# One transformer layer on Trainium2: K's bias added by VectorE in place of a TensorE product per tile and a ScalarE copy

## What is computed

```
h   = layernorm(x) * (1 + ca) + sa
Xn  = layernorm(h) * gamma + beta
Q, K, V = split(Xn @ W_in + b_in)
K, V = rotary(K), rotary(V)                 # first 256 columns
A   = sum over tokens of (K/|K|) * (V/|V|)
Y   = (0.5 * A + 0.5) * Q
x   = x + ga * (Y @ W_out + b_out + h)
x   = x + gb * experts(layernorm(x) * (1 + cb) + sb)   # 8 experts, 2 per token, and a shared one
```

## Time and profile before

| | us |
|---|---|
| median of 3 runs | 775.45 |
| lowest, highest | 774.5, 776.64 |
| the profiled execution, its own time | 775.31 |
| its span in the profile | 773.5 |
| granted clock of TensorE, mean | 0.969 of full speed |

### The profile page before, as it was taken

How to read it: one execution, slowest core, us unless ns; L and a number is a source line. 1 busy time by engine, 2 the same in 40 slices (tenths; PEclk the granted TensorE clock), 3 DMA queues, 4 the chain that set the end, 5 groups by cost and what they waited for, 6 DMA issues and landing times.

```text
span 773.5 us, 10585 instructions
## 1 busy us (share of the span) xinstructions
PE 718.8 (93%) x3812; PEld 590.2 (76%) x3812; DVE 476.6 (62%) x958; ACT 263.6 (34%) x491; POOL 166.2 (21%) x220
## 2 busy tenths in 40 slices
PE   5799999999787698999999997999999999999993
PEld 1477777778565486788787886889898999989892
DVE  3886688537999934335767745284655747465541
ACT  2455255422454314012012022253443525344330
POOL 1233133200111200000000003114335161533404
PEclk9799999999999989999999997999999999999997
DMA  8921211001376721110410404548376674836415
GB/s 298 354 71 54 83 28 42 15 1 44 134 219 217 247 67 47 55 56 0 127 57 15 133 0 125 169 144 173 114 141 135 149 133 143 170 118 106 54 15 69
DMA packets 44107, 83.57 MB, mean 108 GB/s; under 512 B 6969, under 2 KB 15161, under 8 KB 43522
## 3 DMA queue, kind: packets, MB, share of 16 engines
q1 hardware_dynamic: 35106, 62.06, 24.9%
q0 software_dynamic: 8960, 20.98, 15.4%
HBM read 59.93 MB, written 24.40 MB: 109 GB/s over the span
## 4 chain that ended last, share of the span: by engine, by line
PE 72%; DVE 15%; issue 5%; DMA 3%; ACT 2%; POOL 2%; SPq 1%; ACTq 0%; DVEq 0%; POOLq 0%
PE bank L1471 21%; PE bank L1472 20%; PE bank L1473 20%; PE bank L1710 3%; DVE rows L1149 1%; DVE st L960 1%; DVE hx L1161 1%; PE bank L1589 1%; DVE xt L1168 1%; PE bank L1510 1%; DVE gsel L1384 1%; PE bank L1528 1%; DVE ht L1376 1%; DMA ewst<-in_L_ffn_w_up 1%; PE bank L1483 1%
## 5 line engine op out<-in xcount | busy, mean ns | idle before, releaser
L1471 PE MATMUL bank<-ht,ew 128*128 128x320 f32 (+1 forms) x384 | 118.9, 310 | 0.7 <-DVE bc_c L1391 0.7
L1472 PE MATMUL bank<-ht,ew 128*128 128x320 f32 (+1 forms) x384 | 118.6, 309 | 0.0
L1473 PE MATMUL bank<-ht,ew 128*128 128x320 f32 (+1 forms) x384 | 118.2, 308 | 0.0
L1471 PE MATMUL bank<-xt,sgu 128*128 128x512 f32 x176 | 70.3, 400 | 4.6 <-DVE rows L1149 4.6
L607 POOL DMA_INDIRECT out_rows<-y,si x40 | 62.9, 1572 | 48.6 <-DVE y L1406 33.7
L1471 PEld LDWEIGHTS bank<-ht,ew 128*128 128x128 f32 (+1 forms) x384 | 68.7, 179 | 1.6 <-DVE bc_c L1391 1.0
L1472 PE MATMUL bank<-xt,sgu 128*128 128x512 f32 x176 | 69.6, 395 | 0.0
L1473 PE MATMUL bank<-xt,sgu 128*128 128x512 f32 x176 | 69.5, 395 | 0.0
L1472 PEld LDWEIGHTS bank<-ht,ew 128*128 128x128 f32 (+1 forms) x384 | 68.6, 179 | 0.3
L1473 PEld LDWEIGHTS bank<-ht,ew 128*128 128x128 f32 (+1 forms) x384 | 68.7, 179 | 0.0
L596 POOL DMA_INDIRECT picked<-h_d,gi x40 | 39.6, 990 | 97.4 <-PE bank L1710 86.7
(11 more groups left out here) (282 smaller groups left out, 1533.4 us busy)
## 6 DMA issues: line engine op xcount, KB each, us to landing
xring<-in_L_attn_X SPq DMA_DIRECT2D x32, 256.0 KB, 3.4
ewst<-in_L_ffn_w_gate SPq DMA_DIRECT2D x8, 704.0 KB, 4.5
ewst<-in_L_ffn_w_up SPq DMA_DIRECT2D x8, 704.0 KB, 4.3
slots<-in_L_wmod SPq DMA_DIRECT2D x4, 1024.0 KB, 6.3
x_d<-rows SPq DMA_DIRECT2D x16, 256.0 KB, 3.7
h_d<-hx SPq DMA_DIRECT2D x16, 256.0 KB, 2.0
xrow<-x_d SPq DMA_DIRECT2D x16, 256.0 KB, 2.8
out_rows<-xrow SPq DMA_DIRECT2D x16, 256.0 KB, 2.8
```

Source lines behind the costliest of these rows:

```text
L1471: nc.tensor.matmul(dst, a[0], b[0], start=first, stop=False)
L1472: nc.tensor.matmul(dst, a[0], b[1], start=False, stop=False)
L1473: return nc.tensor.matmul(dst, a[1], b[0], start=False, stop=last)
```

## The change

K's product loses its bias product and ends with the 12th. In tile 0 TensorE makes the bias once, as rows for all partitions, in W_BANK, and ScalarE copies it to `kb` (which lies where the bias pairs were). VectorE's new `k_row(t)` adds it to K's bank and writes `ksb`; ScalarE's `k_row` goes. `k_square` reads `ksb` in place of the bank and waits for it. `k_row(t)` stands in VectorE's turn between tokens_lo(t+1) and x_statistics(t+3). TensorE may write K's bank again when `k_row` has read it.

```diff
@@ -180,6 +180,8 @@
                 prod = al2("prod", [P, 2, 3 * ROT])
                 arow = al2("arow", [P, B, ROT])
                 cs = al2("cs", [P, NB, 2, P])
+                with ExitStack() as row_phase:
+                    kb = region(row_phase)("kb", [P, D])
                 bkv = al2("bkv", [P, 2, D], F32R)
                 mrow = al2("mrow", [P, 2, D])
             u = al("u", [P, 2, D])
@@ -256,6 +258,7 @@
         s0_ready = sem("s0_ready")
         w_hi, w_lo = sem("w_hi"), sem("w_lo")
         bias_mm, bias_hi, bias_ready = sem("bias_mm"), sem("bias_hi"), sem("bias_ready")
+        kb_mm, kb_ready = sem("kb_mm"), sem("kb_ready")
         sincos, sinsq = sem("sincos"), sem("sinsq")
         misc_mm, misc_read = sem("misc_mm"), sem("misc_read")
 
@@ -664,17 +667,11 @@
                     act.wait_ge(misc_mm, MISC.index("mod") + 1)
                 nc.scalar.activation(tokens(t, 0), chunked(bank[T_BANKS[t % 2]][:, :]), ACT.Copy).then_inc(t_hi, 1)
 
-            def k_row(t):
-
-                act.wait_ge(k_mm, t + 1)
-                if t >= 2:
-                    act.wait_ge(multiplied, t - 1)
-                nc.scalar.activation(ksb[:, t % 2, :], bank[K_BANKS[t % 2]][:, :], ACT.Copy).then_inc(k_copied, 1)
-
             def k_square(t):
                 if t:
                     act.wait_ge(v_sq, t)
-                nc.scalar.activation(junk[:, :], bank[K_BANKS[t % 2]][:, :], ACT.Square,
+                act.wait_ge(k_copied, t + 1)
+                nc.scalar.activation(junk[:, :], ksb[:, t % 2, :], ACT.Square,
                                      accum_out=nrm[:, t, 0:1]).then_inc(k_sq, 1)
 
             def v_square(t):
@@ -741,7 +738,9 @@
                     v_square(t - 1)
                 if t == NB + 1:
                     a_rows(0)
-                k_row(t)
+                if t == 0:
+                    act.wait_ge(kb_mm, 1)
+                    nc.scalar.activation(kb[:, :], bank[W_BANK][:, :], ACT.Copy).then_inc(kb_ready, 1)
                 if t + 1 < NT:
                     tokens_hi(t + 1)
                 k_square(t)
@@ -1000,6 +999,17 @@
                 dve.wait_ge(bias_hi, i + 1)
                 dve.scalar_tensor_tensor(bkv[:, i, :], bkv[:, i, :].bitcast(F32), nodd[:, :],
                                          bank[(W_BANK, MISC_BANK)[i]][:, :], ALU.mult, ALU.add).then_inc(bias_ready, 1)
+
+            def k_row(t):
+
+                dve.wait_ge(k_mm, t + 1)
+                if t == 0:
+                    dve.wait_ge(kb_ready, 1)
+                else:
+                    dve.wait_ge(multiplied, t)
+                if t >= 2:
+                    dve.wait_ge(k_sq, t - 1)
+                dve.tensor_tensor(ksb[:, t % 2, :], bank[K_BANKS[t % 2]][:, :], kb[:, :], ALU.add).then_inc(k_copied, 1)
 
             def products(t):
 
@@ -1097,6 +1107,7 @@
                     modulated(t + 2)
                 if t + 1 < NT:
                     tokens_lo(t + 1)
+                k_row(t)
                 if t + 3 < NT:
                     x_statistics(t + 3)
                 if t in (8, 9):
@@ -1515,18 +1526,21 @@
 
                 to = bank[(K_BANKS, V_BANKS)[i][t % 2]][:, :]
                 if t >= 2:
-                    pe.wait_ge((k_sq, v_sq)[i], t - 1)
+                    pe.wait_ge((k_copied, v_sq)[i], t - 1)
                 if i == 0:
                     pe.wait_ge(t_lo, t + 1)
                 for k in range(DC):
                     if t == 0:
                         pe.wait_ge(w_lo, DC * i + k + 1)
-                    product3(to, [tokens(t, s)[:, k, :] for s in range(2)], [wkv[:, s, i, k, :] for s in range(2)],
-                             k == 0, False)
+                    last = product3(to, [tokens(t, s)[:, k, :] for s in range(2)], [wkv[:, s, i, k, :] for s in range(2)],
+                                    k == 0, not i and k == DC - 1)
+                if i == 0:
+                    last.then_inc(k_mm, 1)
+                    return
                 if t == 0:
-                    pe.wait_ge(bias_ready, i + 1)
-                nc.tensor.matmul(to, pairs4[:, :].to_broadcast([P, P]), bkv[:, i, :], start=False, stop=True)\
-                    .then_inc((k_mm, v_mm)[i], 1)
+                    pe.wait_ge(bias_ready, 2)
+                nc.tensor.matmul(to, pairs4[:, :].to_broadcast([P, P]), bkv[:, 1, :], start=False, stop=True)\
+                    .then_inc(v_mm, 1)
 
             def misc(name):
 
@@ -1534,6 +1548,7 @@
                 to = bank[W_BANK if name == "cos_a" else MISC_BANK]
                 if n < 2:
                     pe.wait_ge(bias_ready, 2)
+                    pe.wait_ge(kb_ready, 1)
                 else:
                     pe.wait_ge(misc_read, n)
                 if name in ("s1", "c1"):
@@ -1622,6 +1637,10 @@
             bias_row(1)
             for t in range(NT):
                 kv_matmul(t, 0)
+                if t == 0:
+                    pe.wait_ge(bias_ready, 1)
+                    nc.tensor.matmul(bank[W_BANK][:, :], pairs4[:, :].to_broadcast([P, P]), bkv[:, 0, :],
+                                     start=True, stop=True).then_inc(kb_mm, 1)
                 if t + 1 < NT:
                     transposes(t + 1)
                 for name in SLOT_A.get(t, ()):
@@ -1631,7 +1650,7 @@
                     misc(name)
                 if t:
                     weighted_sums(t - 1)
-            pe.wait_ge(k_sq, NT - 1)
+            pe.wait_ge(k_copied, NT)
             pe.wait_ge(v_sq, NT - 1)
             pe.wait_ge(t_lo, NT)
             m_matmul(0, (0,))
```

## The result

| | before | after |
|---|---|---|
| median of 20 runs | 773.91 us | 776.34 us |
| lowest, highest | 772.62, 777.2 | 773.7, 778.04 |
| ratio, 95% interval | | 1.0029 [1.0018, 1.004] |
| span of the profiled execution | 773.5 | 774.9 |

The change costs 0.29%, some 2.2 us, with 0.9 us of uncertainty to either side. 777.6 us had been forecast over a median of 775.4, so +2.2. The cost lies just inside the bound of 0.3% that the prediction drew for "same", but its interval leaves out zero: it is small and real.

The account below looks back on a forecast made before the run. TensorE, busy 93% of the span, was taken to set the loop's time. Removed products -3.45, misc bank stall +1.88 and tiles 8 to 14 +3.77 give +2.20 us: 775.4 + 2.2 = 777.6 us, range 773.4 to 780.3.

Parts of the forecast that it names:

- same: Outcome class: measured time within 0.3% of before, 773.1 to 777.8 us; chance 0.43.
- c1's wait: Sign in tile 1: TensorE waits for ScalarE before c1, near 44.5 us, for 1.9 us.
- three waits for tokens_lo: Sign between 120 and 150 us: TensorE waits for VectorE's tokens_lo by 0.7, 1.4 and 1.4 us.
- The gain: K's bias products removed in tiles 1 to 15: 15 x 0.23 = 3.45 us off TensorE.
- Place 1: Misc bank, tiles 1 to 4: B-slot product waits for ScalarE's read behind the square; 1.88 us stall, tiles 2 to 4 0.
- Place 2: Tiles 8 to 14: VectorE's turn grows from 7.44 to 8.36 us against TensorE's 6.94; stalls 3.77 us.
- late weights: Tile 14: weighted_sums(13) comes some 0.19 us late.
- The sum: End of the loop: -3.45 + 1.88 + 3.77 = +2.20 us.
- Carried over whole: Behind the loop: TensorE has no idle time from 158 to 190 us, so all +2.20 us reaches the total.
- (1): Rival: TensorE's clock falls after idle gaps at the loop's start, costing 1.7 us more, 779.3 us; chance 0.22.
- (2): Rival: the square does not hold ScalarE, both places stay hidden, all 3.45 us come through, 772.0 us; chance 0.08.
- (3): Rival: only one place bites; only the second 775.7 us, only the first 773.9 us; chance 0.18 together.

Follow-up runs that it names:

- e1: Kernel before with K's bias product left out in all 16 tiles and nothing in its place (K lacks its bias); ratio to before 0.9966, loop end 154.64 us.
- e2: Changed kernel with ScalarE's read of the A slot's misc bank put ahead of its square of K; ratio to before 0.9992, loop end 158.82 us.
- e9: Same kernel as e1, run again on another chip with the kernel before beside it; ratio to before 0.9949, loop end 154.63 us.
- r1: Second profile, a single execution, of the unaltered changed kernel; loop end 160.92 us, length 123.63 us, no ratio.
- e6: Changed kernel with a bias product kept in K of every tile beside VectorE's addition (K has another value); ratio to before 1.0073, loop end 164.23 us.
- r3: Second profile, a single execution, of e6; loop end 165.0 us, length 127.17 us, no ratio.
- e5: Changed kernel with ScalarE's square of K last in every turn and scaled_q ahead of normed in turns 10 to 13; ratio to before 0.9952.
- e3: Changed kernel with ScalarE's square of K put behind normed and scaled_q in turns 10 to 13 only; ratio to before 0.9992, loop end 159.13 us.
- e4: Changed kernel with ScalarE's square of K put last in every turn; ratio to before 0.9969, loop end 156.93 us.

## Why the prediction was right

Of the signs it named, these came: 16 products with bias rows in the loop and one for K; c1's wait; ScalarE's square waiting for VectorE's new line 16 times, 36.1 us in all; three waits for tokens_lo between 120 and 150 us. K of tile 8 started 0.7 us later than before, not 0.3. c1 waited 1.74 us where 1.9 had been named, and the three waits for tokens_lo were 0.8, 1.1 and 1.1 us where 0.7, 1.4 and 1.4 had been.

- **The gain.** 3.45 us forecast; e1's loop ends 3.61 us sooner, of which its start (K of tile 1 at 37.07 in place of 37.36) is 0.29 and the products 3.3.
- **Place 1.** 1.88 us forecast for c1. From K(1) to K(2) the changed kernel takes 47.95 - 37.28 = 10.67 us; before it was 8.89, less 0.23: 2.01 too long, of which 1.74 shows as idle. The square from SBUF lasted 632 ns and held ScalarE for 0.63 us until its next instruction (45.07 to 45.70); the sum had taken 0.60 for that. Mis-sized: I put 0 into the sum for tiles 2 to 4, and they cost 0.13, 0.07 and 0.12 us. Their B-slot product starts 3.90 to 3.91 us behind the transposes, where I had the chain at 3.86, and lasts 0.07 to 0.12 us longer until the next one. With the read put first (e2) these tiles are 0.13, 0.06 and 0.13 us shorter again.
- **Place 2.** Turn 8.36 forecast, 8.42 measured; K of tiles 12, 13 and 14 late by 0.88, 1.49 and 1.48 us against TensorE's 6.94, 3.85 together, 3.77 forecast. The 0.19 us for late weights is where I erred in place: it stood in tiles 12 and 13 (0.29, 0.26), hidden in the wait for tokens_lo that follows, and not in tile 14. The 1.42 per turn was short by the 0.06 of the turn, half of it the square. Tile 12's 0.74 was short by 0.14: the turn again, and K starting 0.83 us behind the start of tokens_lo (129.86 to 130.69), where I had 0.75.
- **The sum.** +2.20 forecast at the loop's end, +2.67 measured, or +2.75 in length: 0.3 of the difference are tiles 2 to 4, 0.1 each the two places. So the mechanism is right and its sum 0.5 us short; that the measured time shows the same +2.2 is in part luck, since its interval, 1.4 to 3.1 us, holds 2.2 and 2.75 alike.
- **Carried over whole.** This step is not shown. In the profiles the shift is 2.67 us at the loop's end and 1.4 at the end of the span, so 1.3 us were given back behind the loop. But that part of one kernel varies by more: from the loop end to the end of the span e1 takes 615.4 us and e9, the same kernel, 613.5 (before 615.3, changed 614.0, r1 614.1). One piece of it can be seen. Before, ScalarE waits 0.87 us for a transfer, the second piece of the first routed expert's weights, and starts to split it 6.83 us after it was asked for; in the changed kernel it doesn't wait and starts after 5.76. Of the fourteen profiles three have such a wait, before, e6 and r3 (1.0 and 0.8 us), and these are the three with K's bias product in every tile; e1 and e9, without product and addition, start after 5.87 and 5.82. So the wait goes with the product and not with the addition. Why is open, and no experiment was made on it.
- **Rivals.** (1), the clock falling in place 1, did not come: behind the wait of 1.74 us it is granted in full.

```profile
46.00:60.00 14.00, 13.68 (x77) 10.02 (x78) 11.18 (x25) 6.09 (x13) 4.72 (x10) 1.00 0.25 89
```

Here the Trainium skill (TensorE: Matmul & The Clock Gate, Part 1), in its rule that the clock comes down after a longer idleness, agrees with the trace. The stretch in tiles 6 and 7 is another matter: that rule does not give it, since the clock came down there with TensorE busy for 25.00 of 25 us. The prediction did not name this stretch, though the trace before has it, from about 91 to 95 us. (2), the gain without the price, did not come; it is what e5 reaches by another order. (3), one place alone, did not come either, both bit; e2 leaves only place 2, and its interval, -1.6 to 0.3 us, just reaches the +0.3 worked out for that. e3 leaves place 1 and 0.8 us of place 2.

On the price of an operation: the strict sentence of the Trainium skill (VectorE: DVE Perf Modes, The DRAIN you can't avoid), by which the next operation waits until the pipe is empty and the addition would cost 0.69 us, is not what the trace shows. From the addition to VectorE's next start are 0.59 to 0.60 us (37.14 to 37.73).

## What to carry to other kernels

When an operation moves to another engine, look at who waits for its result and what stands behind that waiter in its queue; here a square that nobody needs soon stood ahead of a bank's read and of scaled_q, which other engines waited for. An average of 62% busy says nothing on that, the sum of one turn's chain does (8.36 forecast, 8.42 measured). And a consumer that has become later should be put later in its engine's order: that alone (e4) turned +0.3% into -0.3%, and with scaled_q, which VectorE waits for, put ahead as well (e5), into -0.5%.

## What was not expected of the hardware

With the same 32 single-column products in tile 6 the granted clock of TensorE over 80 to 105 us was 0.93 in some kernels and 0.86 in others, each the same in both profiles where there are two, although e4 and e5 have the same instructions up to there. TensorE was busy throughout. The difference is 1.55 us in tiles 6 and 7, nearly half of the 3.45 us that the removed products are worth, and no edit here explains it. A comparison of two profiles should look at this before it puts 1 or 2 us down to an edit.
